# The deformable convolution of layer 1: each tap's convolution first, its result gathered and summed with pixels as rows

## What is computed

```python
d = pw(dw(x[:, :256]));  d = (d - mean(d)) / sqrt(var(d) + 1e-5)      # per image and channel
off = conv3x3(d, off_w, off_b)                # 18 channels: dy, dx for each of 9 taps
for each tap t, pixel (y, x):                 # deformable convolution, 512 -> 512 channels
    samples[:, t, y, x] = bilinear(d, y + ky(t) + dy, x + kx(t) + dx)      # 4 corners, 0 outside
dc = einsum('bckhw,ock->bohw', samples, dc_w) + dc_b
dc = (dc - mean_c(dc)) / sqrt(var_c(dc) + 1e-5) * ln_g + ln_b              # over channels
out = x * d * sigmoid(dc) + x * g             # g: a gate for each image and channel
```

## Time and profile before

| | us |
|---|---|
| runs, median (lowest to highest) | 4576.61 (4568.99 to 4583.65) |
| profiled execution, its time | 4580.41 |
| its span, first to last instruction | 4578.6 |
| busy PE, DVE, ACT, POOL over the span | 4151.6, 2895.7, 2530.3, 1002.4 |
| layer 1, from the last output of layer 0 to the first DMA of layer 2 | 2874.6 to 3728.4 |
| its sampling, first tile to last | 3050.8 to 3681.6 |

### The profile page before, as it was taken

The page is one execution under the profiler, slowest core; times in us unless marked ns, Lnnn a source line. Parts: engine busy times, 40 slices in busy tenths (PEclk is TensorE's granted clock), DMA queues, the critical chain, the costliest instruction groups (busy, mean ns, idle before and its releaser), DMA issues. The chain is left out here.

```text
span 4578.6 us, 66114 instructions
## 1 busy us (share of the span) xinstructions
PE 4151.6 (91%) x19516; PEld 2350.7 (51%) x19516; DVE 2895.7 (63%) x4233; ACT 2530.3 (55%) x4526; POOL 1002.4 (22%) x691
## 2 busy tenths in 40 slices
PE   2599999999999999999999999469899976969999
PEld 1355555555555555555557777224444432435553
DVE  7877777777777777777765333726667624225652
ACT  3588888888888888888874333211212211113331
POOL 1311111111101101101103555212222200016663
PEclk7799999999999999999999999779999986989999
DMA  1200000000000000000011000088667620363311
GB/s 43 85 2 2 2 2 2 2 2 2 2 2 2 2 2 2 2 2 2 2 35 41 0 0 0 18 325 322 206 231 247 224 75 38 118 165 65 65 38 74
DMA packets 97332, 280.52 MB, mean 61 GB/s; under 512 B 33130, under 2 KB 34154, under 8 KB 78046
## 3 DMA queue, kind: packets, MB, share of 16 engines
q1 hardware_dynamic: 76510, 128.48, 9.3%
q0 software_dynamic: 20736, 151.00, 9.3%
HBM read 224.38 MB, written 54.85 MB: 61 GB/s over the span
## 5 line engine op out<-in xcount | busy, mean ns | idle before, releaser
L572 DVE SCALAR_TENSOR_TENSOR cpb_r<-cpb_z,cpb_r 128x512 fp32r<-128x512 f32 x2052 | 1322.0, 686 | 491.6 <-ACT cpb_r L547 485.9
L547 ACT ACTIVATE cpb_r<-cpb_z 128x512 fp32r<-128x512 f32 x2052 | 1120.9, 604 | 279.3 <-PE cpb_z L479 279.3
L553 ACT ACTIVATE cpb_h<-cpb_z,net_vec 128x512 f32<-128x512 f32 x1536 | 1020.5, 714 | 0.8 <-PE cpb_z L495 0.8
L492 PE MATMUL cpb_z<-cpb_r,cpb_w2a 128*128 128x512 f32 x2048 | 856.2, 418 | 3.0
L493 PE MATMUL cpb_z<-cpb_r,cpb_w2b 128*128 128x512 f32 x2048 | 803.1, 392 | 0.0
L495 PE MATMUL cpb_z<-cpb_r,cpb_w2a 128*128 128x512 f32 x2048 | 796.8, 389 | 0.0
L430 POOL TENSOR_TENSOR cpb_exp<-l0k_posx,l0k_pos 128x1024 bf16 (+1 forms) x130 | 247.5, 1904 | 1966.5 <-PE cpb_z L479 1946.3
L1322 PE MATMUL dc_pc<-dc_sc,l_dcw 128*128 128x512 f32 x1152 | 532.8, 607 | 6.5 <-ACT dc_dc L1377 6.5
L492 PEld LDWEIGHTS cpb_z<-cpb_r,cpb_w2a 128*128 128x128 f32 x2048 | 383.9, 187 | 189.7 <-issue 123.3
L504 PE MATMUL cpb_zo<-cpb_h,cpb_w3w 128*32 128x512 f32 x3584 | 477.3, 605 | 0.0
L495 PEld LDWEIGHTS cpb_z<-cpb_r,cpb_w2a 128*128 128x128 f32 x2048 | 385.0, 188 | 85.1
(11 more groups left out here) (319 smaller groups left out, 4534.5 us busy)
## 6 DMA issues: line engine op xcount, KB each, us to landing
corners<-cf_tt SPq DMA_DIRECT2D x77, 256.0 KB, 3.6
qk_parts<-gn_r SPq DMA_DIRECT2D x64, 256.0 KB, 2.0
l_dcw<-in_dc_wT SPq DMA_DIRECT2D x9, 1024.0 KB, 11.2
bias_dram<-cpb_bst SPq DMA_DIRECT2D x520, 8.0 KB
net_x<-in_x SPq DMA_DIRECT2D x8, 1024.0 KB, 8.8
sa_qa<-qk_parts SPq DMA_DIRECT2D x16, 512.0 KB
sa_ka<-qk_parts SPq DMA_DIRECT2D x16, 512.0 KB
l_w<-in_mlp_w1T SPq DMA_DIRECT2D x1, 4096.0 KB, 23.3
```

The source lines that it names most:

```text
L492: pe.matmul(z2[:, bank, :], W2A[:], R1[:, k, :], start=True, stop=False)
L547: act.activation(R1[:, t % RING, :], z1[:, t % 4, :], ACT.Relu).then_inc(r1_ready, 1)
L553: act.activation(H2[:, t % 8, :], z2[:, t % 3, :], ACT.Relu, bias=V("cpb_b2")).then_inc(h2a, 1)
L572: v.scalar_tensor_tensor(R2[:, t % RING, :], z1[:, t % 4, :], 0.0, R1[:, t % RING, :].bitcast(F32), ALU.max, ALU.subtract).then_inc(r2_rea ...
```

## The change

The two blocks become one, `layer1`, written out without loops. The table of corners, the transposes of samples and the products with ones go. The three products of a tap are now taken for all pixels first: d is split into DH (high, ACT) and DL (low, DVE), each tap's weights into WH (ACT) and WL (POOL), two taps deep, in the memory of X, which is written out to DRAM at the start and read back at the end. PE makes for each of 18 units (a tap and an image; ORDER) 8 tiles of 128 pixels by 512 output channels, 12 instructions each. ACT copies a tile from PSUM to a ring of 4 (YS), and SP stores it with 4 DMAs of 64 KB into one of 3 x 2 tables in DRAM (by tap modulo 3, and image), whose borders were zeroed. POOL gathers for each tile with two indirect DMAs of 128 rows of 4 KB (two neighbouring pixels of the row above, and of the row below) into a ring of 4 (G). DVE adds four weighted corners to the sum of all taps (ACC), all four with scalar_tensor_tensor. With pixels as rows the channel statistics are bn_stats on DVE; the normalised rows are turned by PE (16 x 4 transposes), and the outputs follow. POOL adds DH and DL to d again in the last two units (whole).

```diff
-def layer1_front(nc, d, g):
...
-                sp.wait_ge(t_ready, i + 1)
-                for k, shift in enumerate(SHIFT):
...
-def layer1_deform(nc, d, g):
...
-                    v.tensor_scalar(o, G[:, k % RING, 0, :], WT[:, 0, col], None, ALU.mult).then_inc(part, 1)
...
-                    mm = pe.transpose(pt[:, k % 2, c, :], SI[:, k % 2, c * P:(c + 1) * P], ident[:])
...
-                    mm = pe.matmul(pc[:, m, :], DCW[:, tap, k, m * P:(m + 1) * P], SC[:, tap % 3, k, :],
...
+def layer1(nc, d, g):
...
+        CHUNKS = HW // P
...
+        SLOTS, GR, YR = 3, 4, 4
...
+        OUT = s.sb("out", [P, CT, NF])
+        WH, WL = WX[:, 0], WX[:, 1]
...
+        table = [[nc.dram_tensor(f"conv_out{u}{b}", (HP * HP, C), F32).ap() for b in range(B)] for u in range(SLOTS)]
...
+        ORDER = [(tap, b) for tap in range(TAPS - 2) for b in range(B)] + [(tap, b) for b in range(B)
+                                                                         for tap in range(TAPS - 2, TAPS)]
...
+            sp.dma_start(x_spill, X[:].rearrange("p t n -> p (t n)")).then_inc(spilled, 16)
...
+            def weights(tap):
+                if tap:
+                    sp.wait_ge(wh_ready, tap)
+                    sp.wait_ge(wl_ready, tap)
+                sp.dma_start(WR[:], d["dc_wT"].rearrange("t (k p) o -> t p k o", p=P)[tap]).then_inc(wr_in, 16)
+
+            weights(0)
+            sp.wait_ge(zeroed, 4)
...
+            for u in range(SLOTS):
+                for b in range(B):
+                    rows = table[u][b]
+                    sp.dma_start(rows[0:edge, :], ZERO[0:edge, :]).then_inc(borders, 16)
+                    sp.dma_start(rows[HP * HP - edge:, :], ZERO[0:edge, :]).then_inc(borders, 16)
+                    middle = rows[edge + W:edge + W + gaps * HP, :].rearrange("(y x) c -> y x c", x=HP)[:, 0:4, :]
...
+            weights(1)
+            weights(2)
+            for i, (tap, b) in enumerate(ORDER):
+                if tap >= SLOTS:
+                    sp.wait_ge(sampled, (PLACE[tap - SLOTS, b] + 1) * CHUNKS)
+                pixels = table[tap % SLOTS][b].rearrange("(y x) c -> y x c", x=HP)
+                for c in range(CHUNKS):
+                    j = i * CHUNKS + c
+                    sp.wait_ge(ys_ready, j + 1)
+                    for y in range(4):
+                        sp.dma_start(pixels[2 + c * 4 + y, 2:2 + W, :], YS[y * W:(y + 1) * W, j % YR, :]).then_inc(stored[j % YR], 16)
+                    if b == 0 and c == 0 and 0 < tap < TAPS - 2:
+                        weights(tap + 2)
+            sp.wait_ge(y_mm, TILES)
+            sp.dma_start(X[:].rearrange("p t n -> p (t n)"), x_spill).then_inc(x_back, 16)
...
+            def weights_low(tap):
+
+                pool.wait_ge(wh_ready, tap + 1)
+                if tap >= 2:
+                    pool.wait_ge(y_mm, tap_tiles(tap - 2))
+                pool.tensor_tensor(WL[:, tap % 2], WR[:], WH[:, tap % 2].bitcast(F32), ALU.subtract).then_inc(wl_ready, 1)
+
+            def whole(b, c):
+
+                m, cols = c % 4, slice(b * HW + c // 4 * NF, b * HW + (c // 4 + 1) * NF)
+                pool.wait_ge(y_mm, (PLACE[TAPS - 1, b] + 1) * CHUNKS)
+                pool.tensor_tensor(DF[:, m, cols], DH[:, m, cols].bitcast(F32), DL[:, m, cols].bitcast(F32), ALU.add
+                                   ).then_inc(d_whole, 1)
+
+            weights_low(0)
+            weights_low(1)
+            pool.wait_ge(idx_ready, 1)
+            pool.wait_ge(borders, 16 * 3 * SLOTS * B)
+            for i, (tap, b) in enumerate(ORDER):
+                for r in range(YR):
+                    pool.wait_ge(stored[r], 64 * (i + 1) * CHUNKS // YR)
+                for c in range(CHUNKS):
+                    u = i * CHUNKS + c
+                    n, q = b * 2 + c // 4, c % 4
+                    col = (n * TAPS + tap) * 4 + q
+                    if u >= GR:
+                        pool.wait_ge(sampled, u - GR + 1)
+                    pool.nop(nofuse=True)
+                    for y in range(2):
+                        pool.indirect_dma_start(out=G[:, u % GR, y, :], out_offset=None, in_=table[tap % SLOTS][b],
+                                                in_offset=bass.IndirectOffsetOnAxis(ap=IDX[:, y, col:col + 1], axis=0)
+                                                ).then_inc(gathered[u % GR], 16)
+                    if i >= len(ORDER) - 2:
+                        whole(i - len(ORDER) + 2, c)
+                if b == 0 and tap + 2 < TAPS:
+                    weights_low(tap + 2)
+
...
+            for k in range(CT):
...
+                        mm = pe.matmul(po[32 * n:32 * n + 32, :], OFW[:, k, tap, :],
...
+            for i, (tap, b) in enumerate(ORDER):
+                pe.wait_ge(wh_ready, tap + 1)
+                pe.wait_ge(wl_ready, tap + 1)
+                for c in range(CHUNKS):
+                    j = i * CHUNKS + c
+                    pixels = slice(b * HW + c * P, b * HW + (c + 1) * P)
+                    if j >= CT:
+                        pe.wait_ge(ys_ready, j - CT + 1)
+                    for k in range(CT):
+                        pe.matmul(py[:, j % CT, :], DH[:, k, pixels], WH[:, tap % 2, k, :], start=(k == 0), stop=False)
+                        pe.matmul(py[:, j % CT, :], DH[:, k, pixels], WL[:, tap % 2, k, :], start=False, stop=False)
+                        mm = pe.matmul(py[:, j % CT, :], DL[:, k, pixels], WH[:, tap % 2, k, :],
+                                       start=False, stop=(k == CT - 1))
+                    mm.then_inc(y_mm, 1)
+
+            for n in range(NT):
+                for q in range(4):
+                    pe.wait_ge(normed, n * 4 + q + 1)
+                    for m in range(CT):
+                        if q == 0 and n:
+                            pe.wait_ge(sig, (n - 1) * CT + m + 1)
+                        mm = pe.transpose(pn[:, m, q * P:(q + 1) * P], ACC[:, n * 4 + q, m * P:(m + 1) * P], ident[:])
+                mm.then_inc(n_mm, 1)
...
+            def weights_high(tap):
+
+                act.wait_ge(wr_in, 16 * (tap + 1))
+                if tap >= 2:
+                    act.wait_ge(y_mm, tap_tiles(tap - 2))
+                act.copy(WH[:, tap % 2], WR[:]).then_inc(wh_ready, 1)
...
+            weights_high(0)
...
+            for b in range(B):
+                for m in range(CT):
+                    act.wait_ge(d_ready, b * CT + m + 1)
+                    act.copy(DH[:, m, b * HW:(b + 1) * HW].rearrange("p (h w) -> p h w", h=H),
+                             DP[:, m, b, 2:2 + H, 2:2 + W]).then_inc(dh_ready, 1)
+            weights_high(1)
...
+                act.wait_ge(l_mv, n * 4 + 4)
+                act.activation(LR[:, n, :], LM[:, n, :, 1], ACT.Sqrt, bias=V("eps5")).then_inc(l_std, 1)
+                act.wait_ge(l_shift, n + 1)
+                for q in range(4):
+                    act.activation(ACC[:, n * 4 + q, :], ACC[:, n * 4 + q, :], ACT.Identity, scale=LR[:, n, q:q + 1],
+                                   bias=LN[:, n, q:q + 1]).then_inc(normed, 1)
...
+                    act.activation(OUT[:, m, :], pn[:, m, :], ACT.Sigmoid, bias=V("ln_b", m), scale=V("ln_g", m)
...
+            for i, (tap, b) in enumerate(ORDER):
+                for c in range(CHUNKS):
+                    j = i * CHUNKS + c
+                    act.wait_ge(y_mm, j + 1)
+                    if j >= YR:
+                        act.wait_ge(stored[j % YR], 64 * (j // YR))
+                    act.copy(YS[:, j % YR, :], py[:, j % CT, :]).then_inc(ys_ready, 1)
+                if b == 1 and tap + 2 < TAPS:
+                    weights_high(tap + 2)
+            for n in range(NT):
+                deviations(n)
+                gates(n)
...
+            for b in range(B):
+                for m in range(CT):
+                    v.wait_ge(dh_ready, b * CT + m + 1)
+                    v.tensor_tensor(DL[:, m, b * HW:(b + 1) * HW].rearrange("p (h w) -> p h w", h=H),
+                                    DP[:, m, b, 2:2 + H, 2:2 + W],
+                                    DH[:, m, b * HW:(b + 1) * HW].rearrange("p (h w) -> p h w", h=H).bitcast(F32),
+                                    ALU.subtract).then_inc(dl_ready, 1)
...
+            v.tensor_copy(IDX[:, 0, :], A["fy"][:]).then_inc(at, 1)
+            v.tensor_scalar(IDX[:, 1, :], A["fy"][:], float(HP), None, ALU.add).then_inc(at, 1)
+            n += 2
+            v.wait_ge(at, n)
+            v.sem_inc(idx_ready, 1)
...
+            def sample(u, tap, b, c):
+
+                n, q = b * 2 + c // 4, c % 4
+                col = (n * TAPS + tap) * 4 + q
+                o = ACC[:, n * 4 + q, :]
+                v.wait_ge(gathered[u % GR], 32 * (u // GR + 1))
+                for k in range(4):
+                    if k:
+                        v.wait_ge(part, u * 3 + k)
+                    v.scalar_tensor_tensor(o, G[:, u % GR, k // 2, (k % 2) * C:(k % 2 + 1) * C], WT[:, k, col:col + 1],
```

(53 more changed lines are left out.)

349 lines of the change are left out of this document (84 added, 265 removed).

## The result

The changed kernel takes **4469.6 us** (median of 4 runs, 4468.6 to 4472.6) against 4577.8 (median of 4, 4569.0 to 4583.7) for the kernel before, a ratio of 0.977 with a 95% interval of 0.975 to 0.978. Forecast were 4487, 4410 to 4575, and faster with 0.79. Its profiled execution took 4470.45 us, 110 less than that of before; layer 1 ends at 3621.6 where it ended at 3728.1, 106.5 us earlier. The last 3.5 us lie in the layers behind it, whose code is the same (847.0 against 850.5 us).

A forecast was written before the change was run, and what follows sets the result against it. PE, the bound before, was to give way to DVE, POOL and DMA at 382, 395 and 397 us. 3051 + 431 + 142 + 14 = 3638, 90 us earlier, gave 4487 us; range 4410 to 4575.

The forecast's parts named there:

- The clock rival: PE's clock stays near 0.50 after gaps in its bursty work, and the kernel takes 4700 us; chance 0.05.
- The front: Stretch before the first sample: 17 us gained are spent on convolving and storing the first unit; first sample at 3051.
- The middle: The 112 tiles of taps 0 to 6: 3.85 us a tile, 431 us in all.
- DVE 382: DVE's work in the 112 tiles: 3.09 us a tile plus 5.1 us for each of seven weight splits, 382 us.
- POOL 395: POOL's work in the 112 tiles: two gather issues, 3.1 us a tile, plus seven weight splits, 347 + 48 = 395 us.
- DMA 397: Transfers in the 112 tiles: gathers and weights at 414 GB/s, stores at 363, 299 + 98 = 397 us.
- The loss by imperfect overlap: In the 112 tiles DVE, POOL and DMA do not overlap perfectly: 3.85 us a tile taken, perfect overlap 3.54.
- The last 32 tiles: Units of taps 7 and 8: 25 us, 38 us, 75 us for the last two, and 4 for what shows, 142 us.
- The tail: After the last sample: statistics, shift, scalings, transposes, sigmoids and products, 14 us (estimate, 10 to 25).
- Smooth overlap: The 112 tiles take 3.54 us each or 3.1 to 3.4, kernel 4430 to 4453 or 4405; chance 0.12.
- Mixed traffic: All transfers of the 112 tiles go at the stores' 352 GB/s: 453 us, 493 with loss, kernel 4549; chance 0.19.
- The round trip: A gather-ring slot's sampling, issues and landing set the pace; slower than before from a 12.5 us landing, 4625 at 14; chance 0.14.

The follow-up runs named there:

- float32_whole: The changed kernel with one plain float32 product in place of three fp32r ones, without the splits, weights loaded four taps ahead: 4448.5 us, 0.972 of before.
- few_stores_three_corners: The changed kernel without the stores of the last six taps and with the fourth corner left out of the sum: 4408.4 us, 0.964 of before.
- three_corners: The changed kernel with DVE adding three of four corners, the fourth still gathered: 4451.4 us, 0.973 of before.
- no_split: The changed kernel without POOL's subtraction of the weights' low parts for the seven later taps: 4453.0 us, 0.974 of before.
- ring_5: The changed kernel with five places in place of four in the ring of gathered tiles: 4449.6 us, 0.973 of before.
- vector_split: The changed kernel with later weight loads, evenly spread stores, a gather ring of five and the weights' low parts subtracted on DVE: 4441.0 us, 0.971 of before.

## Why the prediction came out as it did

**What bounds.** Right: PE left the path and the next three users decide. The forecast's "nobody makes it wait" holds for PE's products alone: its transposes waited 61.8 us for DVE. **PE**: taken 2.72 us a tile, measured 2.80 (22.4 us a unit). It started the convolution at 3010.5 (forecast about 3013), its first instructions 0.42 us apart where later ones come 0.23 apart; the granted clock was 0.50 to 3012, 0.85 to 3014 and 1.00 from there, about as forecast. The clock rival didn't come: 0.91 in the middle, with 0.50 only in PE's six stops there and a few us behind each (0.50 from 3132 to 3140, PE standing from 3126.5 to 3136.5). The cheaper product, by which the forecast took PE off the path, was not needed for the gain: in float32_whole PE takes 3.46 us a tile, just above the bytes' 3.31, and the kernel is 21 us faster than the change.

**The front.** First sample 3047.2, forecast 3051. The first issue waits 25.6 us for the stores of the first unit, so the 17 us gained ahead were mostly spent there, as said.

**The middle, 413.5 against 431.** Term by term:
- DVE 382: measured 346 + 31 = 377. The row of the MLP gave a stop of 5.1 us a split; it was 4.5.
- POOL 395: too high by 40 to 50. few_stores_three_corners bounds it at 112 x 2.78 + 7 x 4.6 = 343 us, and with the mean issue of the change, 1.13 us, it is 112 x 2.86 + 32 = 352. The step that failed was taking the 1.25 us of an issue beside a busy DVE for all issues, and as work of POOL: it is 0.94 us of work and the rest a wait for the end of a DVE instruction. In the change 217 of the 288 issues took more than 0.96 us, and 200 of these ended within 0.03 us of the end of a DVE instruction; in three_corners, with DVE idler, the median issue is 0.94 (1.18 in the change). A split cost 4.6, not the 6.9 of the MLP's median.
- DMA 397: the mis-sized term that carries the error. 155.9 MB at 412 GB/s are 378 us, 19 less, and 431 - 413.5 is 17.5. The 19 us are two errors of about the same size. I priced the stores by the row in which they went alone, 352 GB/s; beside gathers the mix went at 412. And I had 159.4 MB, with the stores of 136 tiles in the middle; 119 tiles were stored there, since 12 were issued ahead of it and 13 behind it. At my own prices the fewer bytes alone give 387.
- The loss by imperfect overlap, 34 us without any row: it was 35 (413.5 - 378). The size was a lucky choice, the kind was not wrong: 21 of the 35 belong to the seven splits, as no_split (-21) and ring_5 (-21) show. Vector_split, with a ring of five and even stores, takes 31.5 away. What the 14 us are that both no_split and ring_5 leave was not taken apart.

**The last 32 tiles.** 148.4 against 142: (7,0) 26.3, (8,0) 40.3, the last two units 81.8 for 75 + 4. DVE's instructions there took 1.83 to 1.96 us in 13 places beside POOL's sums of d, 0.75 elsewhere, 15 us in all; one tile of four instructions with such a place, where others take 3.08:

```profile
3516.52 4.17 DVE L1365 SCALAR_TENSOR_TENSOR dc_acc<-dc_g,dc_wt,dc_acc 128x512 f32<-128x512 f32 x4
```

I had these sums as POOL's load only, though the row for DVE's loss was at hand. That their removal would give the 15 us was not tried. **The tail**: 12.5 for 14, the shift took a round trip of 0.5 us and not 2.3.

**The rivals.** Smooth overlap (3.54 us a tile or less) didn't come by itself; the ring of five reaches 3.51, vector_split 3.41. Mixed traffic at the stores' rate falls, 412 against 352. The Trainium skill (DMA: Bandwidth & Descriptors, Where 436 GB/s comes from) gives a limit of about 358 GB/s for transfers between HBM and SBUF; on this one core the 412 lie above it, and the measurement decides. The round trip is real in kind and small: landings of 7.9 us in the median, far from the 12.5 at which it would have made the kernel slower, cost 21 us with a ring of four.

In sum the end came at 3621.6 for 3638, of which the middle is 17.5, the front 4, the last tiles -6.5 and the tail 1.5.

## What to carry to other kernels

Price a resource by a row in which it does the mix that it will have, count the bytes that fall into the stretch, and tell work from waiting in a row's duration before you multiply it by a count. When two users are level (here DVE with 377 and DMA with 378 us), cutting one alone can show little (2 us for DVE's, 24 for the stores', 41 for both): cut both, or look for what makes each of them pause, here one subtraction on the engine that issues the gathers. Before adding a cheaper form of a product, see whether its preparation sits on an engine that others wait for.

## What the runs showed of the hardware

- Gathers and stores of opposite direction together moved 412 GB/s with the engines full (share 1.04), more than stores alone, 352.
- A GpSimd subtraction of two 128x2048 operands in SBUF (4.5 to 4.65 us) held one VectorE instruction for all its length, 5.2 us for 0.75. The other way round VectorE's 2.28 us subtraction held a GpSimd DMA issue, 2.26 for 0.94. Beside each of the seven subtractions one issue took 1.90 to 2.68 us. The Trainium skill (SBUF — State Buffer, Who interferes with whom) has the first: a VectorE instruction with two SBUF inputs contends with a GpSimd one that reads SBUF, and the shared port pair is an exclusive lock. The rows agree. For the second the same section infers that a tensor_tensor does not hold up the writing of descriptors; the seven issues in vector_split were held, and the measurement decides.
- The same bytes land later when more are in flight: the median from issue to landing between 3078 and 3400 us was 8.3 us with a ring of four and 9.9 with five, while the middle got 21 us shorter. So a longer landing time did not mean a slower middle here.
